# Four attention layers on one core: the max shifts of layers 0 and 2 are spread in another PSUM bank, kept twice, and the written-out order is renewed

## The chip, the cores and the metric

One core of a Trainium2 chip runs the whole program. The time is that of one execution on the device in microseconds; the result is the median of several. Beside it stands one profiled execution of the same kernel, whose trace gives every instruction's start and duration.

## The reference, cut to what matters

Thirty-two images of 128 channels by 1024 pixels pass through four layers, each of them attention over the pixels of one image:

```python
x = _L0_conv_ref(x, ...)   # group norm, one head of 128 channels, softmax over 1024 keys, residual
x = _L1_conv_ref(x, ...)   # group norm, eight heads of 16 channels, softmax, projection, residual
x = _L2_conv_ref(x, ...)   # instance norm, one head of 128 channels, softmax, residual
x = _L3_conv_ref(x, ...)   # linear attention, no softmax
```

Layers 0 and 2 ("full" layers, names with f) compute, for each image,

```python
attn = softmax(q k^T * C**-0.5)   # 1024 x 1024
out  = attn v
```

The softmax subtracts each query's largest score before the exponential. The change touches how that subtraction is done, not what it computes.

## The kernel before, in words

**Stages.** The work on one image is cut into 661 steps. Each step is a few instructions on one engine, and a step's name says its layer: g_ (norm of layer 0), f_ (layers 0 and 2, with the layer as last argument), p_ (norm and projections of layer 1), m_ (the maxima of layer 1), s_ (scores, exponential and values of layer 1), o_ (its division and projection), i_ (norm of layer 2), t_ (layer 3). TensorE, VectorE, ScalarE, GpSimd and the DMA queue of SyncE each play their own steps strictly in order.

**The order is written out by hand.** TIME has a number for every step, PERIOD (line 31) is the distance between two images, and a step of image i comes at i * PERIOD plus its number. STEPS_IN_ORDER sorts all of them once, and each engine takes its own steps out of that list (play). So in the steady state one period holds steps of four or five neighbouring images in a fixed interleaving, and the numbers act only through the order they give. What an engine really waits for is a semaphore in front of each step.

**The banks.** PSUM has eight banks, and each is given to one purpose: P_HEAD (two banks, a score tile of layer 1), P_MAX (two banks, the tiles whose maxima VectorE reduces, for layer 1 by m_max and m_max_read, for the full layers by f_max and f_max_read), P_ACC (values of layer 1), P_SC (score tiles of the full layers), P_FULL (values of the full layers) and P_CHAIN (everything short: projections, averages, spreads). Nothing is double-buffered: a tile can be written when the one before it has been read. P_CHAIN's readers are counted in the semaphore chain, by a table that is built from the order (CHAIN_READER, chain_free, chain_left).

**The full layers' shifts.** f_max computes a 128 x 1024 score tile for 128 queries, and f_max_read reduces it to one column of f0mx or f2mx. After four such columns f_shift (GpSimd, line 742) writes them on the diagonals of f_diag. f_base (TensorE) multiplies f_diag by a matrix of ones, which spreads the negated maxima of the 512 queries of one half over all partitions, into P_SC. f_based (VectorE, line 1087) copies that to f_shifts. Only then may f_scores write the first score tile of the half into the same bank. f_less (line 1107) adds f_shifts to a tile on its way to fp, f_exp (ScalarE, lines 892 and 894) takes the exponential twice, f_plo (GpSimd, line 760) makes the low part, f_add (lines 777 and 781) sums, and f_pv multiplies by the values. There are two halves (h = 0, 1) of eight tiles each (u = 0 to 15), for each of the two layers. The base of half 1 waits for the eighth f_less of half 0, since it overwrites both P_SC and the one f_shifts.

**The DMA queue** (SyncE) plays load, stack (six transfers that lay layer 1's q and k out by heads, one stack for each two pairs of heads), m_row, o_gather, o_move, o_return, f_gather, f_return and store, in order too; a transfer whose semaphore isn't reached holds up all behind it. f_out (GpSimd, line 787) writes x3 and waits for the store of the image before.

All matmuls of the program are recorded on line 1251, so the tiles tell them apart: p_sc<-f_diag,ones_r is f_base, p_sc<-f2q_hi,f2k_hi begins an f_scores of layer 2, p_chain<-zrow,ones_r is a spread of reciprocals, p_chain<-cw,t_dn is t_turn.

## Time and profile before

| | us |
|---|---|
| median of 3 runs | 6187.82 (6186.03 to 6192.17) |
| profiled execution, its time | 6179.77 |
| profiled execution, its span | 6178.0 |
| one period in the steady state (store to store, 27 of 31) | 182.3 to 183.2 |
| TensorE busy | 5741.7 (93%) |
| VectorE busy | 4620.2 (75%) |
| ScalarE busy | 4141.6 (67%) |
| GpSimd busy | 3426.0 (55%) |

TensorE's busy time is a union of modelled matmul durations: a matmul's record is longer than the distance to the next one, so waits shorter than that overlap are not visible as idle time. The distance from one record's start to the next is the better measure of what a step takes. The last periods are shorter (169, 147, 158 and 135 us), since fewer images are in flight.

### The profile page before, as it was taken

The page shows a single profiled execution, that of the slowest core. Times are in us where ns is not written, and L with a number is a line of the kernel's source. Part 1 is how long each engine was busy: PE and PEld are TensorE (multiplying, and loading weights), DVE is VectorE, ACT ScalarE, POOL GpSimd, SP SyncE. Part 2 cuts the span into 40 slices and gives each one's busy share as a digit, 9 for nine tenths or more (in the row PEclk, how much of TensorE's full clock was granted, in tenths as well). Part 3 has the DMA queues.
Part 4 walks back from the last instruction along what each step waited for, and adds up shares of the span by engine and source line. Part 5 has one row for each costly group of instructions (what it writes and reads, how often), then busy time and mean ns, then how long its engine had stood idle before and what let it go on. Part 6 is the DMA issues. An engine that isn't in the chain of part 4 may idle for free.

```text
span 6178.0 us, 82441 instructions
## 1 busy us (share of the span) xinstructions
PE 5741.7 (93%) x28818; PEld 2690.0 (44%) x28818; DVE 4620.2 (75%) x5748; ACT 4141.6 (67%) x5764; POOL 3426.0 (55%) x2739
## 2 busy tenths in 40 slices
PE   5789999999999999999999999999999999999885
PEld 2334444444444444444444444444444444444332
DVE  2677777777777777777777777777777777777752
ACT  2367777766777676777766767767677777677652
POOL 4336655556665555655555666555565555566433
PEclk7899999999999999999999999999999999999996
DMA  1011101011101101111101110110110110111000
GB/s 36 4 27 24 29 21 30 20 31 24 31 19 30 31 20 31 24 25 25 29 21 31 24 31 19 30 30 21 31 24 21 29 30 20 31 24 31 16 17 8
DMA packets 103485, 154.27 MB, mean 25 GB/s; under 512 B 63776, under 2 KB 66080, under 8 KB 102944
## 3 DMA queue, kind: packets, MB, share of 16 engines
q1 hardware_dynamic: 103072, 149.00, 11.1%
q8 instruction: 230, 3.77, 0.3%
q14 instruction: 183, 1.50, 0.1%
HBM read 18.13 MB, written 16.78 MB: 6 GB/s over the span
## 4 chain that ended last, share of the span: by engine, by line
PE 72%; DVE 16%; ACT 5%; issue 3%; POOL 3%; DMA 0%; SPq 0%; DVEq 0%; POOLq 0%; ACTq 0%
PE p_max L1251 16%; PE p_chain L1251 15%; PE p_sc L1251 12%; PE p_full L1251 11%; PE p_acc L1251 9%; PE p_head L1251 8%; DVE mx_half L1066 8%; ACT p L930 3%; DVE f2mx L1061 2%; DVE fp L1107 2%; POOL x L787 1%; POOL fsum L781 1%; POOL fp_lo L760 1%; DVE f_num L1125 1%; DVE t_dn L1198 1%
## 5 line engine op out<-in xcount | busy, mean ns | idle before, releaser
L1066 DVE TENSOR_REDUCE mx_half<-p_max 128x2 f32<-128x1024 f32 x2048 | 2506.8, 1224 | 891.1 <-PE p_max L1251 883.1
L930 ACT ACTIVATE p<-p_head 128x1024 f32<-128x1024 f32 x2048 | 2094.8, 1023 | 1103.0 <-PE p_head L1251 1047.8
L760 POOL TENSOR_TENSOR fp_lo<-fp,fp_hi 128x512 fp32r<-128x512 f32 x1024 | 1311.6, 1282 | 734.1 <-ACT fp L894 732.5
L781 POOL TENSOR_TENSOR fsum<-fsum,fp 128x512 f32<-128x512 f32 x768 | 987.9, 1286 | 282.3 <-ACT fp L894 282.1
L1251 PE MATMUL p_max<-ks,qs 63*128 63x512 f32 x4096 | 993.9, 481 | 102.0 <-DVE mx_half L1066 80.3
L1251 PE MATMUL p_acc<-p,v 128*17 128x512 f32 x8192 | 1080.9, 601 | 7.8 <-ACT p L930 7.6
L1251 PE MATMUL p_head<-qs,ks 64*128 64x512 f32 x4096 | 938.9, 454 | 43.6 <-ACT p L930 26.5
L892 ACT ACTIVATE fp_hi<-fp 128x512 fp32r<-128x512 f32 x1024 | 641.4, 626 | 367.3 <-DVE fp L1107 261.6
L1107 DVE TENSOR_TENSOR fp<-p_sc,f_shifts 128x512 f32<-128x512 f32 x1024 | 700.1, 684 | 147.5 <-PE p_sc L1251 60.3
L1251 PEld LDWEIGHTS p_max<-ks,qs 63*128 63x128 f32 x4096 | 385.8, 185 | 921.5 <-DVE mx_half L1066 736.3
L1251 PEld LDWEIGHTS p_head<-qs,ks 64*128 64x128 f32 x4096 | 385.7, 185 | 679.5 <-issue 385.8
L894 ACT ACTIVATE fp<-fp 128x512 f32<-128x512 f32 x1024 | 634.2, 619 | 0.0
L1061 DVE TENSOR_REDUCE f0mx<-p_max 128x1 f32<-128x1024 f32 x256 | 312.2, 1220 | 136.4 <-PE p_max L1251 136.2
L777 POOL TENSOR_TENSOR fsum<-fp 128x512 f32<-128x512 f32 x128 | 164.1, 1282 | 427.6 <-ACT fp L894 427.6
L1061 DVE TENSOR_REDUCE f2mx<-p_max 128x1 f32<-128x1024 f32 x256 | 312.5, 1221 | 104.2 <-PE p_max L1251 104.2
L1251 PEld LDWEIGHTS p_acc<-p,v 128*17 128x17 f32 x8192 | 144.6, 95 | 328.3 <-issue 282.2
L1251 PE MATMUL p_sc<-f2q_hi,f2k_hi 128*128 128x512 f32 x512 | 253.6, 495 | 35.0 <-DVE fp L1107 31.3
L1251 PE MATMUL p_sc<-f0q_hi,f0k_hi 128*128 128x512 f32 x512 | 251.0, 490 | 19.9 <-DVE fp L1107 17.9
L1251 PE MATMUL p_full<-fp_hi,f0v_hi 128*128 128x512 f32 x512 | 242.6, 474 | 2.7 <-POOL fp_lo L760 2.7
L1251 PE MATMUL p_full<-fp_hi,f2v_hi 128*128 128x512 f32 x512 | 228.7, 447 | 5.9 <-POOL fp_lo L760 5.9
L1251 PE MATMUL p_max<-f2k_hi,f2q_hi 128*128 128x512 f32 x512 | 187.7, 448 | 29.2 <-DVE f2mx L1061 17.4
L1251 PE MATMUL p_max<-f0k_hi,f0q_hi 128*128 128x512 f32 x512 | 185.2, 444 | 24.8 <-DVE f0mx L1061 17.2
(187 smaller groups left out, 7977.6 us busy)
## 6 DMA issues: line engine op xcount, KB each, us to landing
qs<-cq_hi SPq DMA_DIRECT2D x128, 256.0 KB, 4.8
ks<-ck_hi SPq DMA_DIRECT2D x128, 256.0 KB, 4.7
x_in<-x_dram SPq DMA_DIRECT2D x32, 512.0 KB, 4.4
qs<-cq_lo SPq DMA_DIRECT2D x64, 256.0 KB, 4.4
ks<-ck_lo SPq DMA_DIRECT2D x64, 256.0 KB, 5.1
out_dram<-x SPq DMA_DIRECT2D x32, 512.0 KB, 5.3
o<-o SPq DMA_DIRECT2D x256, 32.0 KB, 2.0
zrow<-rz SPq DMA_DIRECT2D x128, 16.0 KB
```

The lines of the kernel that those rows point to most:

```text
L760: pool.tensor_tensor(fp_lo[u % 2][:, :], fp[u % 2][:, :], f32(fp_hi[u % 2][:, :]), ALU.subtract).then_inc(f.plo, 1)
L777: pool.tensor_tensor(dst, fp[(u - 1) % 2][:, :], fp[u % 2][:, :], ALU.add)\
L781: pool.tensor_tensor(dst, dst, fp[u % 2][:, :], ALU.add).then_inc(f.sum, 1)
L787: pool.tensor_tensor(x3[:, :], f_num[:, :], x2[:, :], ALU.add)\
L892: act.activation(fp_hi[u % 2][:, :], fp[u % 2][:, :], ACT.Exp, scale=float(C) ** -0.5).then_inc(f.p, 1)
L894: act.activation(fp[u % 2][:, :], fp[u % 2][:, :], ACT.Exp, scale=float(C) ** -0.5).then_inc(f.pexact, 1)
L930: act.activation(p1[slot][:, 2 * pr:2 * pr + 2, :], P_HEAD[:, :].rearrange("p (e n) -> p e n", e=2), ACT.Exp, scale=float(DH) ** -0.5).the ...
L1061: dve.reduce_max(f_mx[layer][:, v:v + 1], P_MAX[:, :], AX.X).then_inc(sem.max_read, 1)
L1066: dve.reduce_max(mx_half[:, pr, :, t, kh], P_MAX[:, :].rearrange("p (e n) -> p e n", e=2), AX.X)\
L1107: dve.tensor_tensor(fp[u % 2][:, :], P_SC[:, :], f_shifts[:, :], ALU.add)\
L1125: dve.tensor_tensor(f_num[:, q], f_num[:, q], P_CHAIN[:, :], ALU.mult)\
L1251: return pe.matmul(dst, lhsT, rhs, start=start, stop=stop)
```

## The change

Five things are changed at once:

1. f_base writes P_CHAIN instead of P_SC, as one more user in that bank's turn, and f_based copies from there. The semaphore f_based is gone; chain takes its place.
2. f_shifts becomes two tiles, one for each half. The second lies on four weight matrices that are not read after the start (wp0, wp1, wp1a, wp1b; the list of matrices is reordered so that they are neighbours).
3. f_scores of a half's first tile no longer waits for the shifts. It waits, like the others, for the read of the tile before it. f_less of the first tile waits for the shifts.
4. f_base of half 1 no longer waits for the last f_less of half 0; f_based waits that its copy's readers in the layer before are done.
5. All numbers of TIME are new, and so is PERIOD; FIRST and FINAL become zero.

```diff
-PERIOD = 206.000
+PERIOD = 205.571
...
-    f_base=[-265.857, 261.032, -234.29, 310.141],
-    f_based=[-267.09, 255.678, -238.322, 303.472],
...
+    f_base=[189.564, 714.532, 231.86, 761.493],
+    f_based=[189.253, 709.867, 225.951, 758.072],
...
-                    f_spread="f_divide", o_spread="o_divide", o_project="o_residual",
+                    f_spread="f_divide", f_base="f_based", o_spread="o_divide", o_project="o_residual",
...
-FIRST = [-0.019, -0.019, -0.003]
-FINAL = [0.012, 0.017, 0.028]
+FIRST = [0.000, 0.000, 0.000]
+FINAL = [0.000, 0.000, 0.000]
...
-        f_shifts = sb("f_shifts", [C, HALF])
+        f_shifts = [sb("f_shifts", [C, HALF]), cw[:, COL["wp0"]:COL["wp0"] + HALF]]
...
             def f_based(b, h, layer):
                 f = full(layer)
                 dve.wait_ge(f.base, b.at(PER.f_base, h + 1))
-                dve.tensor_copy(f_shifts[:, :], P_SC[:, :]).then_inc(f.based, 1)
+                if layer == 0:
+
+                    after(dve, (sem.f2.less, b.shift(-3), PER.f_less, T * (h + 1)),
+                          (sem.f0.less, b.shift(-1), PER.f_less, T * (h + 1)))
+                else:
+                    after(dve, (sem.f0.less, b.shift(2), PER.f_less, T * (h + 1)),
+                          (sem.f2.less, b.shift(-1), PER.f_less, T * (h + 1)))
+                dve.tensor_copy(f_shifts[h][:, :], P_CHAIN[:, :]).then_inc(sem.chain, 1)
 
             def f_less(b, u, layer):
                 f = full(layer)
                 dve.wait_ge(f.sc, b.at(PER.f_sc, u + 1))
-                dve.wait_ge(f.based, b.at(PER.f_based, u // T + 1))
+                if u % T == 0:
+                    dve.wait_ge(sem.chain, chain_left("f_based", b, u // T, layer))
...
-                dve.tensor_tensor(fp[u % 2][:, :], P_SC[:, :], f_shifts[:, :], ALU.add)\
+                dve.tensor_tensor(fp[u % 2][:, :], P_SC[:, :], f_shifts[u // T][:, :], ALU.add)\
                    .then_inc(f.less, 1)
...
             def f_base(b, h, layer):
                 f = full(layer)
                 pe.wait_ge(f.shift, b.at(PER.f_shift, h + 1))
-                if h:
-                    pe.wait_ge(f.less, b.at(PER.f_less, T))
...
-                mm(P_SC[:, :], ones_r[:, :], f_diag[:, :, :].rearrange("p t c -> p (t c)"))\
-                    .then_inc(f.base, 1)
+                chain_free("f_based", b, h, layer)
+                mm(P_CHAIN[:, :], ones_r[:, :], f_diag[:, :, :].rearrange("p t c -> p (t c)"))\
+                    .then_inc(f.base, 1)
...
             def f_scores(b, u, layer):
...
-                if kt:
+                if u:
                     pe.wait_ge(f.less, b.at(PER.f_less, u))
-                else:
-                    pe.wait_ge(f.based, b.at(PER.f_based, h + 1))
```

The new numbers of TIME are the places 0 to 660 of an order, each used once in a period. What they move is seen in the order of the instructions, at three places that matter below. In all three, the first block is the kernel before and the second the changed one.

TensorE, where half 0 of layer 2 gets its shifts. From the second p_chain<-zrow,ones_r (the spread of reciprocals of layer 0) to the base:

```order
L1251 MATMUL p_chain<-zrow,ones_r 128x512
L1251 MATMUL p_max<-f2k_hi,f2q_hi 128x512 x2
L1251 MATMUL p_head<-qs,ks 128x512 x2
L1251 MATMUL p_acc<-p_0,v_1 17x512 x4
L1251 MATMUL p_head<-qs,ks 128x512 x2
L1251 MATMUL p_max<-f2k_hi,f2q_hi 128x512 x2
L1251 MATMUL p_sc<-f_diag,ones_r 128x512
```

```order
L1257 MATMUL p_chain<-zrow,ones_r 128x512
L1257 MATMUL p_head<-qs,ks 128x512 x2
L1257 MATMUL p_max<-f2k_hi,f2q_hi 128x512 x2
L1257 MATMUL p_sc<-f2q_hi,f2k_hi 128x512
L1257 MATMUL p_sc<-f2q_lo,f2k_hi 128x512
L1257 MATMUL p_sc<-f2q_hi,f2k_lo 128x512
L1257 MATMUL p_head<-qs,ks 128x512 x2
L1257 MATMUL p_acc<-p_0,v_1 17x512 x4
L1257 MATMUL p_max<-f2k_hi,f2q_hi 128x512 x2
L1257 MATMUL p_chain<-f_diag,ones_r 128x512
```

The first score tile of layer 2 (three matmuls), which came after the base with five other steps between, now lies ahead of it.

VectorE, where half 1 of layer 2 begins. The copy of its shifts (COPY f_shifts), the last maxima of layer 1 (mx_half, then mx), the first maxima of layer 0 of a later image (f0mx), the row of negated maxima for layer 1 (CAST neg), and the tiles 8 and 9 of layer 2 (fp):

```order
L1066 TENSOR_REDUCE mx_half<-p_max 128x2
L1087 COPY f_shifts<-p_sc 128x512
L1066 TENSOR_REDUCE mx_half<-p_max 128x2
L1075 TENSOR_TENSOR mx<-mx_half 128x2x2x8
L1061 TENSOR_REDUCE f0mx<-p_max 128x1 x2
L1107 TENSOR_TENSOR fp<-p_sc,f_shifts 128x512
L1061 TENSOR_REDUCE f0mx<-p_max 128x1
L1082 CAST neg<-p_chain 32x128
L1107 TENSOR_TENSOR fp<-p_sc,f_shifts 128x512
```

```order
L1064 TENSOR_REDUCE mx_half<-p_max 128x2
L1092 COPY cw<-p_chain 128x512
L1064 TENSOR_REDUCE mx_half<-p_max 128x2
L1113 TENSOR_TENSOR fp<-p_sc,cw 128x512
L1064 TENSOR_REDUCE mx_half<-p_max 128x2
L1059 TENSOR_REDUCE f0mx<-p_max 128x1
L1073 TENSOR_TENSOR mx<-mx_half 128x2x2x8
L1059 TENSOR_REDUCE f0mx<-p_max 128x1
L1113 TENSOR_TENSOR fp<-p_sc,cw 128x512
L1059 TENSOR_REDUCE f0mx<-p_max 128x1
L1080 CAST neg<-p_chain 32x128
```

The copy moved one reduction ahead, tile 8 moved ahead of the last reduction of layer 1, and tile 9 stands two instructions before CAST neg where it stood right behind it.

The DMA queue, from the load of an image to o_move (o_0<-o_1):

```order
L670 DMA zrow<-f0rz 1x128x8 x2
L614 DMA x_in<-x_dram 128x1024
L675 DMA out_dram<-x 128x1024
L634 DMA qs<-neg 2x16x128
```

```order
L659 DMA f2zt<-cw 128x1x8
L668 DMA zrow<-f2rz 1x128x8 x2
L673 DMA out_dram<-x 128x1024
L653 DMA zrow<-rz 4x32x32 x2
L644 DMA o_0<-o_1 16x512 x4
```

The store (out_dram<-x) stood behind the load and stands behind the return of layer 2's reciprocals (zrow<-f2rz). Everything else in the queue keeps its order.

Two more moves belong to layer 3. On TensorE five steps came between t_matrix (p_chain<-tm,ka) and t_ksum (p_chain<-cw,ma), and now two do. On VectorE tile 9 of layer 0 (fp) stood in front of t_scale (wb, t_dn, t_ds) and stands behind it and the reduction after it.

## Rows read from the trace of the kernel before

**Rows 1.** Page: busy time, share of the span, instructions of each engine

```profile
PE 5741.7 (93%) x28818; PEld 2690.0 (44%) x28818; DVE 4620.2 (75%) x5748; ACT 4141.6 (67%) x5764; POOL 3426.0 (55%) x2739
```

**Rows 2.** Busy time by stretch, one period: us, busy PE, PEld, DVE, ACT, POOL, PEclk, DMA

```profile
2992.40:3175.20 182.80, 176.01 (x903) 83.08 (x901) 144.35 (x181) 129.21 (x181) 106.78 (x86) 1.00 0.12 26
```

**Rows 3.** Who waited for whom: engine, line, releaser, us in total, times, longest

```profile
PEld p_max L1251 <- DVE mx_half L1066: 736.3, 1186, 1.8
...
PEld p_head L1251 <- ACT p L930: 284.1, 389, 1.7
```

**Rows 4.** Timeline of PE, layer 2's base of half 0 (start us, us, what [idle<-releaser])

```profile
3005.26 0.50 PE L1251 MATMUL p_chain<-zrow,ones_r 2*128 2x512 f32 x1
...
3008.52 0.73 PE L1251 MATMUL p_max<-f2k_hi,f2q_hi 128*128 128x512 f32 x2
...
3009.64 0.50 PE L1251 MATMUL p_sc<-f_diag,ones_r 128*128 128x512 f32 x1 [0.38 <-POOL f_diag L742]
...
3012.83 0.48 PE L1251 MATMUL p_sc<-f2q_hi,f2k_hi 128*128 128x512 f32 x1
...
3016.61 0.50 PE L1251 MATMUL p_sc<-f2q_hi,f2k_hi 128*128 128x512 f32 x1 [0.27 <-DVE fp L1107]
```

**Rows 5.** Timeline of DVE, the same stretch

```profile
3005.86 0.69 DVE L1125 TENSOR_TENSOR f_num<-f_num,p_chain 128x512 f32<-128x512 f32 x1 [0.21 <-PE p_chain L1251]
...
3012.26 1.22 DVE L1061 TENSOR_REDUCE f2mx<-p_max 128x1 f32<-128x1024 f32 x1 [0.37 <-PE p_max L1251]
...
3014.30 1.22 DVE L1061 TENSOR_REDUCE f2mx<-p_max 128x1 f32<-128x1024 f32 x1 [0.31 <-PE p_max L1251]
...
3015.86 0.69 DVE L1107 TENSOR_TENSOR fp<-p_sc,f_shifts 128x512 f32<-128x512 f32 x1
```

**Rows 6.** Busy time by stretch, the same stretch (columns as in Rows 2)

```profile
3004.43:3018.28 13.85, 13.02 (x67) 4.86 (x60) 12.74 (x21) 8.93 (x11) 2.85 (x3) 1.00 0.26 77
```

**Rows 7.** Timeline of PE, layer 2's tile 10

```profile
3064.27 0.50 PE L1251 MATMUL p_sc<-f2q_hi,f2k_hi 128*128 128x512 f32 x1 [0.53 <-DVE fp L1107]
```

**Rows 8.** Timeline of DVE, just before it

```profile
3060.95 1.23 DVE L1061 TENSOR_REDUCE f0mx<-p_max 128x1 f32<-128x1024 f32 x1 [0.22 <-PE p_max L1251]
3063.34 0.28 DVE L1082 CAST neg<-p_chain 32x128 fp32r<-32x128 f32 x1 [1.16 <-PE p_chain L1251]
3063.55 0.67 DVE L1107 TENSOR_TENSOR fp<-p_sc,f_shifts 128x512 f32<-128x512 f32 x1
```

**Rows 9.** Timeline of PE, layer 3

```profile
3126.08 1.83 PE L1251 MATMUL p_chain<-tm,ka 128*17 128x129 f32 x15
...
3131.06 0.39 PE L1251 MATMUL p_chain<-cw,ma 17*128 17x17 f32 x2
...
3134.21 1.05 PE L1251 MATMUL p_chain<-cw,t_dn 128*17 128x128 f32 x8 [0.68 <-DVE t_dn L1209]
```

**Rows 10.** Chain that ended last: one step of P_MAX's ring

```profile
3082.86 0.45 PE p_max L1251 x2
3083.33 1.24 DVE mx_half L1066
3084.61 0.51 PE p_max L1251 x2
```

**Rows 11.** Timeline of the DMA queue: return of layer 2, then a stack's last transfer

```profile
3096.74 1.17 SPq L670 DMA_DIRECT2D zrow<-f2rz  x2
...
3144.57 1.30 SPq L629 DMA_DIRECT2D ks<-ck_lo  x1
```

**Rows 12.** Timeline of POOL: f_out

```profile
3108.03 2.39 POOL L787 TENSOR_TENSOR x<-f_num,x 128x1024 f32<-128x1024 f32 x1 [0.34 <-DVE f_num L1125]
```

**Rows 13.** Page: a stack's transfers, KB each, us to landing

```profile
ks<-ck_lo SPq DMA_DIRECT2D x64, 256.0 KB, 5.1
```

**Rows 14.** Timeline of PE: the tile that waits for this stack

```profile
3151.05 0.50 PE L1251 MATMUL p_max<-ks,qs 63*128 63x512 f32 x2
```

**Rows 15.** One tile (x): transfers of 512 KB, issue to landing

```profile
DMA to landing us min/median/max: 2.6/5.3/5.7
```

More of the change, by code:

```diff
@@ L158 @@
-    o_return=[50.299, 119.226],
-    o_move=[88.54, 101.005],
-    o_spread=[215.825, 217.853],
-    o_divide=[215.329, 218.256],
-    o_project=[220.642, 226.102],
-    o_residual=[226.176, 228.408],
-    i_stat=[230.18],
-    i_apply=[235.791],
-    f_out=[374.775],
-    t_project=[371.091, 374.67, 375.592],
-    t_tokens=[372.077, 374.541, 377.951],
-    t_norms=[379.422],
-    t_keys=[380.954],
-    t_matrix=[390.878],
-    t_keep=[376.906],
-    t_ksum=[395.741],
-    t_scale=[390.327],
-    t_turn=[396.761, 400.053],
@@ new lines @@
+    p_lo=[309.61, 323.605, 323.916, 339.466],
+    p_value=[324.849, 328.581],
+    p_keep=[323.294, 325.16],
+    stack=[268.558, 339.155],
+    m_max=[378.652, 380.829, 383.006, 384.872, 386.738, 388.915, 391.092, 394.202, 396.69, 399.489,
[6 rows of a table added]
+    m_max_read=[374.92, 376.786, 377.097, 380.518, 381.451, 389.537, 390.47, 390.781, 396.068,
[6 rows of a table added]
+    m_both=[455.469, 555.611],
+    m_turn=[462.311, 572.716],
+    m_neg=[460.445, 561.831],
+    m_row=[362.791, 421.57],
+    s_scores=[465.11, 467.598, 470.086, 471.641, 473.818, 476.617, 478.794, 482.837, 485.014,
[6 rows of a table added]
@@ new lines @@
+    o_recip=[579.869, 666.327],
+    o_return=[499.631, 585.778],
+    o_move=[527.932, 568.051],
+    o_spread=[672.858, 674.102],
+    o_divide=[671.303, 676.59],
+    o_project=[676.901, 679.078],
+    o_residual=[683.121, 684.054],
+    i_stat=[684.987],
+    i_apply=[686.231],
+    f_out=[828.98],
+    t_project=[830.846, 833.645, 839.243],
+    t_tokens=[825.248, 832.09, 836.755],
+    t_norms=[841.109],
+    t_keys=[844.53],
+    t_matrix=[853.549],
+    t_keep=[846.085],
+    t_ksum=[856.97],
@@ L250 @@
     f_base = 2
-    f_based = 2
     f_less = 2 * T
@@ L325, in __init__ @@
         self.base = new(f"f{layer}_base")
-        self.based = new(f"f{layer}_based")
         self.less = new(f"f{layer}_less")
```

156 lines of the change are left out of this document (73 added, 83 removed), and 48 rows, old and new, of tables (m_max, m_max_read, s_exp, s_scores).

## The prediction

> **What bounds the kernel now.** I read the page first, for the shares [rows 1]: TensorE is busy 93% of the span, VectorE 75%, ScalarE 67%, GpSimd 55%. Then one steady period by itself [rows 2]: 182.8 us, TensorE busy 176.0, VectorE 144.4, ScalarE 129.2, GpSimd 106.8, at a granted clock of 1.00. TensorE's 176 is not all work, because a matmul's record runs on after the next has started: the scores of a full tile are three records of about 0.4 us that start 0.23 to 0.34 apart. So I looked at who waited for whom [rows 3]. The weight loads for p_max waited 736 us for VectorE's reductions and those for p_head 284 us for ScalarE's exponentials. The kernel is a fixed interleaving on TensorE with many small gaps (736 us in 1186 waits, 0.6 us each); a change in the order pays where it fills a gap, and costs where it opens one.
>
> No instruction goes and none comes: four bases, four copies and 32 score tiles for each image before and after. The copy reads 128x512 from one bank instead of another, and I take it at the same price. Everything is therefore waits. I went to the places where the old rule (the base sits in P_SC, the first tile waits for the copy) or the moved steps touch a visible gap.
>
> **Place one, the base of half 0 of layer 2.** The second spread starts at 3005.26 and the base at 3009.64 after an idle wait for GpSimd's f_diag; those 4.38 us are a chain through VectorE and GpSimd, not TensorE work [rows 4]. The first score tile starts at 3012.83, and the second only at 3016.61, after a wait for VectorE's fp. The changed order puts the first tile (three matmuls, 0.8 us from start to start) into the stretch before the base, where TensorE has time. That takes 0.8 us out of what follows. But VectorE is nearly full here: its gaps ahead of the first fp are 0.21, 0.37 and 0.31 us [rows 5], and over the 13.85 us around it VectorE is busy 12.74 [rows 6]. Only the last two gaps wait for tiles that TensorE now sends earlier, so at most 0.37 + 0.31 = 0.68 us can be had. I take **0.65 us**, the two idle waits of TensorE, 0.38 and 0.27 [rows 4]; from below 0.
>
> **Place two, tile 10 of layer 2.** It starts after an idle wait of 0.53 us for fp of tile 9 [rows 7]. VectorE stood idle 1.16 us in front of CAST neg, whose matmul was late, and fp was queued behind it [rows 8]. In the changed order fp comes two instructions ahead of the cast, and its score tile one value tile earlier, because the base of half 1 no longer has to wait for the bank and the single f_shifts. The wait goes: **0.53 us**; from below 0.
>
> **Place three, layer 3.** t_turn waits 0.68 us for t_dn [rows 9]. t_matrix starts at 3126.08 and t_ksum, which starts t_dn's chain, at 3131.06. With two steps between them instead of five, and with fp of tile 9 behind the chain instead of before it (0.68 us), t_dn is ready about 1 us sooner and the wait goes: **0.68 us**. The fp that was passed is needed by a tile some 10 us later, so the delay is covered; without that cover it would cost the chain's 2.7 us.
>
> **The other three bases** (both of layer 0, half 1 of layer 2) show no idle wait on TensorE, since many other steps lie between their maxima and their use; I count them at nothing. If a base now came before its f_diag, TensorE would wait as it does for half 0 of layer 2, 0.38 us each.
>
> **What the new order costs.** P_MAX is one tile deep. From one tile to the next is 0.47 + 1.28 = 1.75 us at best [rows 10], and TensorE needs that much other work in between. I added up, over the 80 pairs of neighbouring tiles of a period, how much work is missing by the steps' own start-to-start times. The sum is 5.8 us in the old order and 6.2 in the new one, 0.4 us more. The tiles of the full layers take 0.73 us instead of 0.50 [rows 4] and so ask for more; I take 0.7. The same count for p_head (1.55 us from tile to tile) gives 2.7 and 1.9, so 0.8 less. These are sums of separate shortfalls, most of which overlap with others. I let the P_MAX debit stand in full and take the p_head credit as nothing, because its exponentials are rarely what the next step in line waits for.
>
> **The sum.** 0.65 + 0.53 + 0.68 - 0.7 = 1.16 us an image; I take **1.0**, since a step that starts sooner meets the next fixed chain. Such chains are the stacks: the last transfer is issued at 3144.57 [rows 11] and lands 5.1 us later [rows 13], at 3149.7, and the tile that needs it starts at 3151.05 [rows 14], only 1.4 us of slack; the new order moves that tile one step forward. The places occur in all 32 images, but the first and the last are less crowded; I count 30: 30 us. On the profiled execution that is 6179.8 - 30 = 6150. The median of the runs stands 8 us above that execution, so against it I say 6187.8 - 30 = **6158 us**, 0.5% less. Bounds for this case: 0.4 us (12 us in all, 6176) if half of the gains meet other chains, and 1.9 (57 us, 6131) if the debit is nothing.
>
> **A rule beside the row.** The P_SC bank is held by base and copy for 0.50 + 0.68 us, four times an image, but it carries 32 tiles of about 1.7 us, some 60 us of 182.8 with the bases: it is idle two thirds of the time, so freeing it is worth no more than the waits above. The Trainium skill (PSUM — Partial Sum Buffer, "PSUM bank collisions raise a hardware error") says that two engines may not use one bank at once, in the same quadrant, and that software must keep them apart. By that rule alone all 4.7 us an image would be exclusion in TensorE's path and the change worth 140 us.
>
> **The rivals.**
> *Given back (0.22).* The waits move instead of going. Place one is limited by VectorE, place two's TensorE meets the f0mx tiles next, and m_max waits for a stack with little slack [rows 13, 14]. For it: VectorE's 12.74 of 13.85 us [rows 6]. Against: place three has nothing behind it. Net 0 to 0.3 us an image: 6180 to 6188.
> *P_MAX decides, slower (0.14).* In the new order a P_MAX tile follows another with only 0.9 us of work in between once (at layer 2's projections), and 1.0 once (f_max 5 to 6 of layer 2), where the least had been 1.1. The 736 us of waits for these reductions [rows 3] are 23 us an image, so this ring is the most waited for. If each shortfall counts and each pushes VectorE's later steps behind it once more, 2 x 0.7 = 1.4 us, and the three places give only 0.4: 1.0 us an image worse, 6218. It decides as soon as the added waits pass the 1.9 us of gains.
> *The store holds up f_out (0.03), slower.* The store now goes out after zrow<-f2rz, whose issue ends at 3097.9 [rows 11]; f_out waits for it and starts at 3108.03 [rows 12]. A 512 KB transfer lands after 5.3 us, at most 5.7 [rows 15]: 3103.6. There are 4.4 us to spare; each us beyond them would cost 30 us, since fp_lo stands behind f_out on GpSimd. A landing of 12 us would give 6158 + 2.3 x 30 = 6227.
> *Freed bank (0.03), much faster.* The exclusion of the rule above counts whole: 6050.
>
> The forecast has 0.58. A measurement of this kernel can tell about 0.2% (12 us) from no change. Faster by more than that is nearly all of the forecast and the freed bank, 0.59; within it 0.23; slower 0.18. The range takes in the forecast's bounds, all of "given back" with the runs' spread, and stops short of the P_MAX case: 6122 to 6203.
>
> **What would show it.** The base of half 0 of layer 2 as p_chain<-f_diag with the first score tile just before it, and the idle waits for f_diag and fp there gone or under 0.3 us. The 0.53 us wait ahead of tile 10 gone, and PE's 21 us of waits for t_dn near zero. A period of 181.5 to 182.2 us. Wrong would be: weight loads of p_max waiting over 750 us for mx_half (the P_MAX rival), f_out released by a DMA (the store), or the same gaps one step later (given back).

## The result and the profile after

| | us |
|---|---|
| median of 3 runs, before | 6187.82 |
| median of 3 runs, changed | 6114.58 (6112.51 to 6120.84) |
| ratio | 0.9883 [0.987, 0.9896], 73 us less |
| profiled execution, its time | 6120.84 (before 6179.77) |
| profiled execution, its span | 6119.0 |
| period in the middle of the run (first score tile of layer 1 to the next image's), median of 17 | 180.3 (before 182.8) |
| the same, mean | 180.58 (before 182.83) |

The forecast was 6158 with a range of 6122 to 6203. The direction was right and the size was not: 73 us came instead of 30, and the result lies 7 us outside the range.

The page of the changed kernel, busy time, against [rows 1]:

```profile
PE 5733.8 (94%) x28818; PEld 2703.8 (44%) x28818; DVE 4583.2 (75%) x5748; ACT 4154.7 (68%) x5764; POOL 3432.1 (56%) x2739
```

One period of it (columns as in [rows 2], TensorE first):

```profile
2939.78:3120.05 180.27, 175.23 (x901) 83.20 (x900) 142.79 (x180) 129.51 (x181) 106.92 (x86) 1.00 0.12 26
```

The same number of matmuls, at the same granted clock of 1.00, and nearly the same busy time: the 2.5 us are idle time that went. Who waited for whom (columns as in [rows 3]):

```profile
PEld p_max L1257 <- DVE mx_half L1064: 614.4, 1016, 1.8
PEld p_head L1257 <- ACT p L928: 331.9, 480, 2.1
...
PEld p_chain L1257 <- DMA zrow<-f2rz: 35.1, 31, 6.1
...
PE p_chain L1257 <- DVE t_dn L1215: 1.9, 1, 1.9
```

Weight loads for p_max waited 122 us less for VectorE than in [rows 3], those for p_head 48 us more for ScalarE, and a new wait for a DMA came, 35 us. TensorE's waits for t_dn are gone.

**Place one** (timeline of TensorE, columns as in [rows 4]). The first score tile now stands ahead of the base, and the base, in p_chain, starts without an idle wait. But a tile of P_MAX behind it now waits for VectorE, and the second score tile still waits for its fp:

```profile
2974.47 0.49 PE L1257 MATMUL p_chain<-zrow,ones_r 2*128 2x512 f32 x1
...
2975.89 0.40 PE L1257 MATMUL p_sc<-f2q_hi,f2k_hi 128*128 128x512 f32 x1
...
2978.86 0.50 PE L1257 MATMUL p_chain<-f_diag,ones_r 128*128 128x512 f32 x1
...
2982.76 0.73 PE L1257 MATMUL p_max<-f2k_hi,f2q_hi 128*128 128x512 f32 x2 [0.58 <-DVE f2mx L1059]
...
2985.83 0.50 PE L1257 MATMUL p_sc<-f2q_hi,f2k_hi 128*128 128x512 f32 x1 [0.26 <-DVE fp L1113]
```

From the second spread to the second score tile it is 11.36 us now and was 11.35 [rows 4]: place one gave nothing.

**Place two.** TensorE around half 1 of layer 2: the base, tile 8 right behind it, a projection of layer 0 (which writes p_chain too), tile 9 and tile 10:

```profile
3020.35 0.39 PE L1257 MATMUL p_chain<-f_diag,ones_r 128*128 128x512 f32 x1
...
3021.78 0.50 PE L1257 MATMUL p_sc<-f2q_hi,f2k_hi 128*128 128x512 f32 x1
...
3022.58 1.02 PE L1257 MATMUL p_chain<-x_in,cw 128*128 128x512 f32 x2
...
3028.04 0.39 PE L1257 MATMUL p_sc<-f2q_hi,f2k_hi 128*128 128x512 f32 x1
...
3032.36 0.40 PE L1257 MATMUL p_sc<-f2q_hi,f2k_hi 128*128 128x512 f32 x1
```

Tile 10 starts without the 0.53 us of [rows 7]. VectorE in the same stretch: the copy of the base, the subtraction of tile 8, that of tile 9, the cast neg, and the maximum behind it:

```profile
3021.17 0.68 DVE L1092 COPY cw<-p_chain 128x512 f32<-128x512 f32 x1
...
3023.09 0.69 DVE L1113 TENSOR_TENSOR fp<-p_sc,cw 128x512 f32<-128x512 f32 x1
...
3029.38 0.68 DVE L1113 TENSOR_TENSOR fp<-p_sc,cw 128x512 f32<-128x512 f32 x1
...
3031.47 0.28 DVE L1080 CAST neg<-p_chain 32x128 fp32r<-32x128 f32 x1
3032.56 1.23 DVE L1059 TENSOR_REDUCE f0mx<-p_max 128x1 f32<-128x1024 f32 x1 [0.81 <-PE p_max L1257]
```

In [rows 8] the cast came after an idle wait of 1.16 us and one subtraction stood between it and the next maximum. Now the cast has no wait before it.

**Place three.** t_matrix starts at 3094.56 and t_ksum at 3097.08, 2.5 us behind it instead of 5.0 [rows 9], and t_turn no longer waits.

```profile
3094.56 1.93 PE L1257 MATMUL p_chain<-tm,ka 128*17 128x129 f32 x16
...
3097.08 0.39 PE L1257 MATMUL p_chain<-cw,ma 17*128 17x17 f32 x2
```

**Where in the period the time went.** I followed TensorE's instructions through both traces by counting them in order, from the first score tile of layer 1 of an image. (s_scores(r, u) is score tile u, 0 to 15, of round r, 0 to 3; a round is four of the eight heads for one half of the queries.) Two orders can be compared only at points up to which both have issued the same instructions. Elsewhere a difference tells what moved and not what was gained: s_scores(1,14) is only 0.06 us earlier, because the changed kernel has the three matmuls of tile 8, 0.8 us, behind it by then and the kernel before has not. At points where the work done is the same (median of 17 images):

| up to | earlier by, us | of it since the row above |
|---|---|---|
| second spread, the start of place one | 0.27 | 0.27 |
| s_scores(1,2), behind place one | 0.27 | 0.00 |
| s_scores(1,12) | 0.73 | 0.46 |
| s_scores(2,0), behind place two | 1.32 | 0.59 |
| s_scores(3,2) | 1.31 | 0.0 |
| s_scores(3,7), ahead of the base of half 1 of layer 0 | 1.86 | 0.55 |
| s_scores(3,12), behind that base | 1.97 | 0.11 |
| s_scores(3,15), behind place three | 2.70 | 0.73 |

**The gains outside the three places.** The 0.46 and the 0.55 us come where TensorE stood idle before a tile of P_MAX until VectorE had reduced the one before it, and the new order sends another step first. Kernel before, then changed, for each of the two:

```profile
3035.72 0.50 PE L1251 MATMUL p_max<-ks,qs 63*128 63x512 f32 x2 [0.30 <-DVE mx_half L1066]
...
3114.98 0.50 PE L1251 MATMUL p_max<-ks,qs 63*128 63x512 f32 x2 [0.48 <-DVE mx_half L1066]
```

```profile
3004.57 1.05 PE L1257 MATMUL p_acc<-p,v 128*17 128x512 f32 x8
3005.56 0.50 PE L1257 MATMUL p_max<-ks,qs 63*128 63x512 f32 x2
...
3082.59 0.50 PE L1257 MATMUL p_head<-qs,ks 64*128 64x512 f32 x2
3082.93 0.41 PE L1257 MATMUL p_max<-ks,qs 63*128 63x512 f32 x2
```

A third wait of this kind, 0.33 us for f2mx, went from the stretch ahead of the second spread, where p_head now goes first. All three are there in each of the 17 images before, and in none after. The two gains are larger than the idle times shown by 0.1 to 0.2 us; that part is not traced. That the swaps make the gains is read from the traces; no run took one of them alone.

### The profile page after: what moved, and what is told of

The parts are those of the page before. It is cut to its first block, busy times and chain, and to the rows that moved or that the text cites. A ratio compares the mean times of both kernels' runs of the same rounds, so it can differ in the third digit from the quotient of the medians.

```text
span 6119.0 us, 81671 instructions
## 1 busy us (share of the span) xinstructions
PE 5733.8 (94%) x28818; PEld 2703.8 (44%) x28818; DVE 4583.2 (75%) x5748; ACT 4154.7 (68%) x5764; POOL 3432.1 (56%) x2739
## 4 chain that ended last, share of the span: by engine, by line
PE 76%; DVE 15%; ACT 3%; issue 2%; POOL 1%; DMA 1%; SPq 1%; POOLq 0%; DVEq 0%; ACTq 0%
PE p_chain L1257 17%; PE p_max L1257 16%; PE p_sc L1257 12%; PE p_full L1257 11%; PE p_acc L1257 11%; PE p_head L1257 9%; DVE mx_half L1064 8%; DVE f2mx L1059 3%; ACT p L928 2%; DVE fp L1113 1%; DVE f0mx L1059 1%; ACT exact L835 0%; DVE x L1163 0%; POOL fsum L779 0%; DVE f_num L1131 0%
## 5 line engine op out<-in xcount | busy, mean ns | idle before, releaser
L1257 PE MATMUL p_max<-ks,qs 63*128 63x512 f32 x4096 | 972.0, 471 | 79.5 <-DVE mx_half L1064 57.4
L1257 PE MATMUL p_head<-qs,ks 64*128 64x512 f32 x4096 | 966.0, 467 | 30.4 <-ACT p L928 17.9
L1113 DVE TENSOR_TENSOR fp<-p_sc,cw 128x512 f32<-128x512 f32 x512 | 349.2, 682 | 71.3 <-POOL fsum L779 30.3
L1113 DVE TENSOR_TENSOR fp<-p_sc,f_shifts 128x512 f32<-128x512 f32 x512 | 349.8, 683 | 53.4 <-PE p_sc L1257 29.3
```

The costliest lines, as they stand in the source:

```text
L1113: dve.tensor_tensor(fp[u % 2][:, :], P_SC[:, :], f_shifts[u // T][:, :], ALU.add)\
L1257: return pe.matmul(dst, lhsT, rhs, start=start, stop=stop)
```

## The experiments

All are the changed kernel or the one before with the edit shown; times are medians of 4 to 11 runs, ratios are to the kernel before on the same chip (6188 to 6192 us there). The f_ lists of TIME count layers fastest: index 2u is layer 0, 2u + 1 layer 2. A line TIME[...] = ... sets one step's number and so moves that step alone in the order.

### Rules and order apart

**new_rules_old_order**: the changed code with the old numbers. **old_rules_new_order**: the old code with the new numbers, and the first tile of half 0 of layer 2 behind its base again, which the old rule needs. **tile0_back**: the changed kernel with that same tile behind its base, so that it differs from old_rules_new_order in the rules alone.

```diff
+TIME["f_scores"][1] = TIME["p_average"][0] + 2 * PERIOD + 0.1
```

> The changed code with the old numbers (TIME, PERIOD, FIRST, FINAL). Theory A, that the gain of 73 us comes from where steps stand in the new order: the order is the old one, TensorE reaches the base and the first tiles at the old places, so the time stays within 10 us of before, 6178 to 6190. Rival B, that the freed bank and the second place for the shifts give the gain by themselves (waits that go whatever the order): 6130 or less. Between them, 6130 to 6178, both have a part.

> The old code (base in P_SC, one f_shifts, first tile waits for the copy) with the new numbers; only the first tile of layer 2 must stand behind the base again (after p_average), since the old rule cannot run otherwise. Theory A: the order keeps most of its gain without the new rules, at most 0.3 us an image lost for the first tile and 0.3 for half 1's base: 6125 to 6140. Rival B: without the rules the gain is gone, 6175 to 6190. A mixed answer would show a wait for the base or the copy that the old rule brings at half 1 of layer 2.

> The changed kernel with the first score tile of layer 2 back behind the base and p_average. My prediction gave this place 0.65 us an image, which would make it 6134. The changed trace shows only 0.3 us gained up to the end of this stretch, so theory A now says 8 us more, 6123. If VectorE really bounds the stretch, 6115 to 6118.

| | us | ratio |
|---|---|---|
| new rules, old order | 6228.27 | 1.0066 [1.0053, 1.0078] |
| old rules, new order | 6209.49 | 1.0033 [1.002, 1.0046] |
| tile0_back | 6118.77 | 0.9889 [0.9876, 0.9903] |

Neither theory had expected this: each half of the change alone is slower than the kernel before, by 39 and 20 us, and together they are 73 faster. tile0_back shows that place one's tile is worth nothing that can be told: 4 us between medians, on ranges that overlap (6115.54 to 6121.41, and 6112.51 to 6120.84), and its TensorE is at s_scores(1,2) as early as the changed kernel's. Between old_rules_new_order and tile0_back only the rules differ, by 91 us, and the starts differ in two places only: 1.16 us between s_scores(1,12) and (1,14), the base of half 1 of layer 2, and 1.35 us between (3,6) and (3,8), the base of half 1 of layer 0. These are two of the bases that I had counted at nothing. And at the points of equal work old_rules_new_order is as far ahead of the kernel before as the changed kernel is at s_scores(1,12), and it gains the same 0.55 us around (3,6): those gains come from the order alone.

### The second halves' waits

**half1_waits** puts the two waits of the old rule back into the changed kernel, for the second halves alone; bank and places stay.

```diff
                 chain_free("f_based", b, h, layer)
+                if h:
+                    pe.wait_ge(f.less, b.at(PER.f_less, T))
...
+                if u == T:
+                    pe.wait_ge(sem.chain, chain_left("f_based", b, 1, layer))
```

> The changed kernel with the old rule's two waits put back for the second halves alone: the base of half 1 waits for the subtraction of tile 7 of its layer, and the first score tile of half 1 waits for the copy of the base. Bank, two places for the shifts, order and first halves stay as changed. Theory A (the serial chain tile 7, base, copy, tile 8 is what the new rules remove, at the two second halves): 91 us over the changed kernel, 6200 to 6212, with the loss between score groups (1,12) and (1,14) (+1.2 us) and between (3,6) and (3,8) (+1.3 us). Theory B (it is the bank, or the copies' place): within 10 us of 6115.

6204.62 us, 1.0024 [1.0014, 1.0033]: 90 us over the changed kernel (87 by the ratios, which allow for the different chips), as theory A said, with +1.17 us up to (1,14) and +1.35 between (3,6) and (3,8). TensorE's timeline in it, base and tile 8, and VectorE's, the subtraction of tile 7 and the copy:

```profile
3062.62 0.47 PE L1257 MATMUL p_chain<-f_diag,ones_r 128*128 128x512 f32 x1 [0.88 <-DVE fp L1113]
...
3064.16 0.50 PE L1257 MATMUL p_sc<-f2q_hi,f2k_hi 128*128 128x512 f32 x1
```

```profile
3061.79 0.68 DVE L1113 TENSOR_TENSOR fp<-p_sc,f_shifts 128x512 f32<-128x512 f32 x1
3063.12 0.69 DVE L1092 COPY cw<-p_chain 128x512 f32<-128x512 f32 x1 [0.65 <-PE p_chain L1257]
```

Tile 7, its subtraction, base, copy, tile 8: in the new order these stand close together, and under the old rule each waits for the one before. So the two waits alone cost some 90 us in the new order; what the bank as such is worth there is too little to tell (this run and old_rules_new_order are 5 us apart).

### Why the new rules lose in the old order

new_rules_old_order falls behind by 1.54 us in one place, between s_scores(1,12) and (1,14):

```profile
3073.99 0.50 PE L1257 MATMUL p_chain<-f_diag,ones_r 128*128 128x512 f32 x1
3075.74 1.13 PE L1257 MATMUL p_chain<-x_in,cw 128*128 128x512 f32 x2 [1.25 <-DVE cw L1092]
```

The base is now one more user of P_CHAIN, and the old order has f_qk(3) of layer 0 right behind it, which writes the same bank and has to wait for the copy. Two repairs were tried. **base_behind_qk** swaps the two; **base_early** puts the base behind tile 7 and the copy behind its subtraction.

```diff
+TIME["f_base"][3] = TIME["f_qk"][6] + 3 * PERIOD + 0.01
```

```diff
+TIME["f_base"][3] = TIME["f_scores"][15] + 0.01
+TIME["f_based"][3] = TIME["f_less"][15] + 0.01
```

> The changed code in the old order (6228.3) with one step swapped: the base of half 1 of layer 2 behind the layer-0 step f_qk(3) that stood right behind it on TensorE. Theory A (the old order with the new rules is slow because f_qk(3), which writes the chains' bank too, now waits for VectorE's copy of the base, 1.5 us an image): 6184 to 6190. Theory B (the loss is in the turns of the chains' bank elsewhere, or in the extra waits of the copy): 6215 to 6230.

> The changed code in the old order (6228) with the base of half 1 of layer 2 and its copy moved forward: base right behind tile 7 on TensorE, copy right behind the subtraction of tile 7 on VectorE, so that the copy is done before f_qk(3) needs the chains' bank. Theory A (the 1.55 us an image that the new rules lose in the old order is the turn of that bank, which the swap with f_qk(3) only handed on, from a wait for the copy to a wait for f_hi(3)): 6183 to 6192. Theory B (another cost of the rules in this order): 6215 to 6230.

base_behind_qk: 6224.81 us, 1.0058 [1.0046, 1.0071]; theory A's number failed. The swap only hands the wait on, since the base now waits for ScalarE's read of f_qk(3):

```profile
3076.27 0.47 PE L1257 MATMUL p_chain<-f_diag,ones_r 128*128 128x512 f32 x1 [1.45 <-ACT exact L835]
```

base_early: 6185.64 us, 0.9994 [0.9985, 1.0003], no different from the kernel before. So the bank's turn was the whole loss, and the new rules in the old order are worth nothing in themselves.

### Place three

**layer3_back**: t_ksum behind five steps again, and the subtraction of tile 9 of layer 0 ahead of layer 3's chain.

```diff
+TIME["t_ksum"][0] = TIME["f_pv"][14] + 3 * PERIOD + 0.1
+TIME["f_less"][18] = TIME["m_max_read"][24] - PERIOD + 0.1
```

> The changed kernel with t_ksum behind the score tile and value tile that it had been moved ahead of, and tile 9 of layer 0 ahead of t_scale again on VectorE. In the changed trace layer 3's stretch of the period is about 1.1 us shorter than before. Theory A: the wait for t_dn comes back (0.5 to 0.7 us idle on TensorE, 15 to 25 us in all in the trace), and the time rises by 1.1 x 30 = 33 us, to 6148. Rival (the shortening has other causes): under 10 us more, 6115 to 6125.

6149.91 us, 0.9942 [0.9928, 0.9955]: 35 us over the changed kernel, 1.2 us an image by my 30 images. The wait for t_dn is back:

```profile
PE p_chain L1257 <- DVE t_dn L1215: 28.9, 30, 1.9
```

### Place two, from the new order

**tile9_back** undoes one step on VectorE, the subtraction of tile 9 ahead of the cast. **second_half_back** puts tiles 8 and 9 and their subtractions back. **turn_back** moves only m_turn(1), the matmul that the cast reads, behind f_max(3).

```diff
+TIME["f_less"][19] = TIME["m_neg"][1] + PERIOD + 0.1
```

```diff
+TIME["f_scores"][17] = TIME["f_value"][0] + 3 * PERIOD + 0.1
+TIME["f_less"][17] = TIME["f_max_read"][2] + 3 * PERIOD + 0.1
+TIME["f_scores"][19] = TIME["f_pv"][15] + 0.1
+TIME["f_less"][19] = TIME["m_neg"][1] + PERIOD + 0.1
```

```diff
+TIME["m_turn"][1] = TIME["f_max"][6] + 2 * PERIOD + 0.1
```

> The changed kernel with the subtraction of tile 9 of layer 2 put back behind m_neg on VectorE; nothing else moves. Theory A (my term for place two, 0.53 us an image, stands or falls with this step, but in the new order tile 9 is issued 2.8 us earlier and can wait): 6115 to 6132. Theory B (this step is the whole gain of 1.25 us at place two): 6145 to 6155.

> The changed kernel with tiles 8 and 9 of layer 2 put back where the order before had them: tile 8 behind f_value(0) of layer 0, tile 9 behind the sum of tile 7, and their subtractions behind f_max_read(1) and m_neg. Theory A (my term: 0.53 us an image): 6128 to 6134. Theory B (the whole of place two hangs on these tiles being early, 1.25 us an image): 6148 to 6156. If neither, up to 6125, the gain lies with the other steps moved there.

> The changed kernel with one step moved: m_turn(1) behind f_max(3) on TensorE, as before the change. Theory A (m_neg then runs later and holds f_max_read(3) behind it on VectorE): f_max_read(3) 0.6 to 1.0 us later, 6132 to 6145. Theory B (only the subtraction of tile 9 behind m_neg costs, as in tile9_back): 6110 to 6122.

| | us | ratio | loss against the changed kernel |
|---|---|---|---|
| tile9_back | 6140.71 | 0.9924 [0.9911, 0.9936] | 26 |
| second_half_back | 6192.46 | 1.0004 [0.9995, 1.0013] | 78 |
| turn_back | 6181.26 | 0.9986 [0.9977, 0.9995] | 67 |

By the ratios the losses are 25, 75 and 64 us. tile9_back fell between the theories and the other two lost more than either allowed. The losses do not add up: moving two tiles back gives back all that the whole change gained. turn_back shows why one step weighs so much. Of its 2.3 us an image only 0.56 come where m_turn stands; 1.7 come some 11 us later, at o_recip(0). Its timeline of the DMA queue, then of VectorE:

```profile
3063.98 0.61 SPq L632 DMA_DIRECT2D qs<-neg  x1
...
3070.68 1.21 SPq L637 DMA_DIRECT2D zt<-o  x1
```

```profile
3063.67 0.28 DVE L1080 CAST neg<-p_chain 32x128 fp32r<-32x128 f32 x1 [1.15 <-PE p_chain L1257]
...
3074.62 0.35 DVE L1144 RECIPROCAL rz<-zt 128x32 f32<-128x32 f32 x1 [0.61 <-DMA zt<-o]
3075.01 1.15 DVE L1147 CAST rz<-rz 128x32 fp32r<-128x32 f32 x1
3076.19 1.21 DVE L1149 TENSOR_TENSOR rz<-rz 128x32 fp32r<-128x32 f32 x1
3077.33 1.21 DVE L1064 TENSOR_REDUCE mx_half<-p_max 128x2 f32<-128x1024 f32 x1
```

The cast is followed on the DMA queue by the row (qs<-neg), the six transfers of a stack and the gather (zt<-o), issued 6.7 us behind the row; the reciprocal starts 4.0 us after the gather's issue. The chain takes 11.0 us in all three kernels: as medians the cast stands at 93.02, 91.65 and 92.87 us of the period before, after and in turn_back, and the reciprocal at 104.06, 102.64 and 103.85. VectorE plays in order, so m_max_read(0) of the next image waits behind it: 105.54, 103.78 and 106.50. So the wait at the cast is also the start of a chain over SyncE's queue that ends in VectorE. In turn_back the reciprocal is 1.2 us later than in the changed kernel; the other 1.5 us up to m_max_read(0) are the two instructions behind it, 1.15 and 1.21 us long here and 0.2 in most images of the changed kernel (see the last section).

This prices the step in the new order. It is no gain on top against the kernel before: the changed kernel is 1.32 us ahead at s_scores(2,0), before the reciprocal, and 1.32 us ahead at (2,8), behind it. The cast had to come forward with the rest, or the gain would have been lost there.

### Is the long copy on the path?

The copy in the middle of o_recip(0) took 0.93 us on the mean in the kernel before (0.38 to 1.06) and 0.18 in the changed kernel, apart from 2 of 21 images with 1.17 and 1.31. **recip_behind_before** moves o_recip(0) of the old kernel one step later, behind m_max_read(0), clear of GpSimd in most images; **recip_behind_after** moves that of the changed kernel behind m_max_read(1).

```diff
+TIME["o_recip"][0] = TIME["m_max_read"][0] + PERIOD + 0.01
```

```diff
+TIME["o_recip"][0] = TIME["m_max_read"][1] + PERIOD + 0.01
```

> The kernel before with o_recip(0) one step later on VectorE, behind m_max_read(0). In the kernel before, the 128x32 copy in o_recip(0) takes 0.93 us on the mean while GpSimd is at a 128x512 sum, against 0.18 us in the changed kernel where GpSimd idles; behind m_max_read(0) it falls into a hole of VectorE (0.6 us) and mostly clear of GpSimd. Theory A (that lengthened copy is part of what the change took off the path at the end of place two): m_max_read(0) starts 0.4 to 0.7 us earlier, 6165 to 6182. Theory B (the copy's length is not on the path): 6186 to 6196.

> The changed kernel with o_recip(0) two steps later on VectorE, behind m_max_read(1), where GpSimd idles in most periods. In the changed kernel o_recip(0)'s copy takes 0.18 us in most periods and 1.2 to 1.3 in those in which GpSimd starts early; those periods are the ones of 181 to 182 us among the 180.2. Theory A: those long periods go, 6104 to 6112. Theory B (the hole behind m_max_read(1) is too short for the three steps, and they push the maxima that follow): 6114 to 6125.

```profile
3077.02 0.34 DVE L1138 RECIPROCAL rz<-zt 128x32 f32<-128x32 f32 x1
3077.40 0.18 DVE L1141 CAST rz<-rz 128x32 fp32r<-128x32 f32 x1
```

These two rows are VectorE's timeline in recip_behind_before: the copy took 0.18 us in each of the same 21 images, but the time was 6188.90, 1.0002 [0.9993, 1.0011]. The 0.75 us were not on the path there; theory A fell. recip_behind_after took 6114.16 us, 0.9882 [0.9868, 0.9895], as the changed kernel. Its mean period fell from 180.58 to 180.33 us, too little for the runs to tell.

### Place two, from the old order

If the place's own steps make the gain, putting them alone into the old order (new rules, base_early) must give it. Each kernel adds to the one before it:

- **tile8_early**: tile 8 ahead of f_qk(3), its subtraction ahead of m_max_read(63).
- **second_half_early**: tile 9's subtraction behind the first maxima, m_turn(1) and s_scores(1,15) ahead of f_max(3), two exponentials earlier.
- **second_half_whole**: what that left out on TensorE, VectorE and ScalarE.
- **second_half_four**: GpSimd's steps there as well, and s_scores(1,13) ahead of tile 7.

The first block is tile8_early's addition, the second some of what the other three add:

```diff
+TIME["f_scores"][17] = TIME["s_scores"][29] + PERIOD + 0.01
+TIME["f_less"][17] = TIME["m_max_read"][62] + PERIOD + 0.01
```

```diff
+TIME["m_turn"][1] = TIME["f_pv"][15] - PERIOD + 0.01
+TIME["f_less"][19] = TIME["f_max_read"][2] + 3 * PERIOD + 0.01
...
+TIME["f_exp"][15] = TIME["f_hi"][6] + 3 * PERIOD - 0.01
...
+TIME["f_add"][15] = TIME["f_vlo"][0] + 3 * PERIOD - 0.01
```

> As base_early, and tile 8 of layer 2 goes ahead of f_qk(3) on TensorE and its subtraction ahead of m_max_read(63) on VectorE, some 5 us earlier; everything else in the old order. Theory A (what the change gains at the second half of layer 2 is that one subtraction leaves VectorE's dense run of maxima, which sets the pace there): 0.6 to 1.4 us an image under base_early, 6145 to 6170. Theory B (the gain needs the whole new order): within 10 us of base_early.

> The changed code in the old order, with all that the new order does at the second half of layer 2 and nothing else of it: base and copy early as in base_early, tile 8 early as in tile8_early, tile 9 and its subtraction behind the first f_max steps instead of in front of m_neg, m_turn(1) and s_scores(1,15) ahead of f_max(3), and ScalarE's exponentials of tiles 8 and 9 each one step earlier. Theory A (place two's gain is that f_max_read(3) is no longer queued behind m_neg and a subtraction, 0.9 to 1.3 us an image, and tile 8 early only makes room for that): 6145 to 6160, against 6185.6 of base_early and 6204.2 of tile8_early. Theory B (it needs the rest of the new order too): over 6175.

> second_half_early with the steps that it left out: the sum of tile 6 ahead of f_max(1), m_both(1) behind f_max_read(0), the subtraction of tile 10 ahead of f_max_read(4), the exponential of tile 7 ahead of f_hi(3) and that of tile 10 ahead of s_out(1) on ScalarE; so TensorE, VectorE and ScalarE do the second half of layer 2 in the new order, and the rest in the old. Theory A (place two's gain needs its own steps on three engines and nothing else): 6145 to 6160, and m_neg some 1.3 us earlier than in base_early. Theory B (it needs what comes before it in the new order as well): over 6175.

> second_half_whole with GpSimd's part as well: the low half of p and the sum of tiles 6 and 7 of layer 2 ahead of the low halves of layer 0's projections and values, as in the new order, and on TensorE s_scores(1,13) ahead of tile 7. On all four engines the steps around the second half of layer 2 then stand as in the changed kernel, everything else as before. In second_half_whole the subtraction of tile 9 waited until 91.88 us of the period (89.60 in the changed kernel) for GpSimd's sum of tile 7, which stood behind f_vlo(0). Theory A (the gain at place two needs its steps on all four engines, and nothing elsewhere): s_scores(2,0) 1.0 to 1.4 us earlier than before, 6145 to 6160. Theory B (it also needs the earlier part of the period): over 6175.

| | us | ratio |
|---|---|---|
| base_early | 6185.64 | 0.9994 [0.9985, 1.0003] |
| tile8_early | 6204.19 | 1.0026 [1.0016, 1.0037] |
| second_half_early | 6211.95 | 1.0037 [1.0023, 1.0051] |
| second_half_whole | 6215.23 | 1.0043 [1.003, 1.0056] |
| second_half_four | 6162.56 | 0.9961 [0.9948, 0.9975] |

The first step made it 19 us slower, the next two did not help (8 and 3 us more, little over the spread), and the last gave 53 us at once. In second_half_whole the subtraction of tile 9 stands where the new order has it, but GpSimd's sum of tile 7, whose buffer it needs, still stands behind a low part of layer 0's values. VectorE's timeline, then GpSimd's:

```profile
3072.06 0.69 DVE L1113 TENSOR_TENSOR fp<-p_sc,cw 128x512 f32<-128x512 f32 x1 [1.48 <-POOL fsum L779]
```

```profile
3069.42 1.30 POOL L750 TENSOR_TENSOR f0v_lo<-exact,f0v_hi 128x512 fp32r<-128x512 f32 x1 [0.52 <-ACT exact L867]
3070.66 1.30 POOL L779 TENSOR_TENSOR fsum<-fsum,fp 128x512 f32<-128x512 f32 x1
```

In second_half_four the sum comes first, and the subtraction has no wait before it. VectorE's timeline again, then GpSimd's:

```profile
3048.24 0.68 DVE L1113 TENSOR_TENSOR fp<-p_sc,cw 128x512 f32<-128x512 f32 x1
```

```profile
3045.41 1.30 POOL L779 TENSOR_TENSOR fsum<-fsum,fp 128x512 f32<-128x512 f32 x1
3047.16 1.29 POOL L750 TENSOR_TENSOR f0v_lo<-exact,f0v_hi 128x512 fp32r<-128x512 f32 x1 [0.44 <-ACT exact L867]
```

Against the kernel before, at the points of equal work, second_half_four is 0.02 us ahead at s_scores(1,12) and 0.61 at (2,0): 0.59 us gained in between, as much as the changed kernel gains there. So the place's steps on four engines do make that gain, with nothing of the rest of the new order. Theory A had expected more, 1.0 to 1.4 us at (2,0) and 28 to 43 us in the time; it was 0.6 and 25. The last step moved GpSimd's steps and one of TensorE's together; that GpSimd's sum is what counts is read from the wait of 1.48 us that went.

### The new wait for a DMA

The return of layer 2's reciprocals is issued later in the new order, and the spread waits for it, 35 us in all. **row_early** moves the row and the reciprocal forward, **spread_later** moves the spread and its division back.

```diff
+TIME["f_row"][1] = TIME["f_exp"][0] + 3 * PERIOD - 0.05
+TIME["f_recip"][1] = TIME["m_max_read"][10] + 2 * PERIOD + 0.1
```

```diff
+TIME["f_spread"][1] += 0.7
+TIME["f_divide"][1] += 0.35
```

> The changed kernel with f_row(2) ahead of the exponential of tile 0 of layer 0 on ScalarE, and f_recip(2) ahead of the subtraction of tile 1 on VectorE, so that the row is returned some 1.6 us earlier. Theory A (the wait for the returned row, 1.0 us an image, is on the path): 6085 to 6100. Theory B (the next wait takes its place): 6110 to 6120.

> The changed kernel with f_spread(0) of layer 2 two steps later on TensorE (behind s_scores(3,1) and m_max(14)) and its division behind m_max_read(14). Theory A (the new wait for the returned row, 1.0 us an image, is on the path): 6085 to 6100. Theory B (the wait is cover for one that comes next, the P_MAX ring): 6110 to 6120.

row_early: 6115.77 us, 0.9883 [0.9869, 0.9896]; spread_later: 6122.65, 0.9894 [0.9881, 0.9908]. In row_early the wait is gone but for the last image:

```profile
PEld p_max L1257 <- DVE mx_half L1064: 618.4, 1030, 1.8
...
PEld p_chain L1257 <- DMA zrow<-f2rz: 6.1, 1, 6.1
```

The time stayed. The weight loads for p_max waited 4 us longer, in 14 more waits; which wait took the other 25 us I did not find. No kernel of the study is faster than the changed one by more than the runs can tell.

## Why the prediction was wrong

**"I let the P_MAX debit stand in full" is the step that failed: the sum took 0.7 us off, and these waits gave time back.** The weight loads for p_max waited 614 us for mx_half instead of 736, and TensorE's idle waits ahead of three tiles of P_MAX (0.33, 0.31 and 0.48 us an image) went. The stretches around them gave 0.27, 0.46 and 0.55 us, 1.3 us an image, none of it in a place of the sum. Adding up how much work is missing between neighbouring tiles came out 0.4 us worse for the new order, against what happened. It counts the work that stands between two tiles, and says nothing of work that is itself waiting, nor of which shortfall TensorE really stands idle for. That the swaps of neighbours make these gains is read from the traces, and old_rules_new_order has them too; which swap gives how much was not tried. I looked for gains only where the old rule or the listed moves touch a wait, and the new order had closed gaps elsewhere. The count for p_head pointed the wrong way too: it promised 0.8 us less, and its waits rose by 48 us.

**Place one, 0.65: nothing.** Between the second spread and the second tile the time is 11.36 us for 11.35. The wait for f_diag went and a wait of 0.58 us for f2mx came. I had named the reason, VectorE's 12.74 of 13.85 us [rows 6], and taken the upper end all the same.

**Place two, 0.53: 0.59 us, right in place and size.** The wait ahead of tile 10 went, and second_half_four makes the same 0.59 us from this place's steps alone. What the term did not have is how many steps on four engines must stand right for it, and that the late cast also starts the chain to the reciprocal: in the new order one of these steps back costs 26 or 67 us. The reason given, that the base of half 1 no longer has to wait, holds: half1_waits loses 1.17 us here.

**Place three, 0.68: 0.73 us in the trace, 1.2 by layer3_back.** The wait for t_dn went. Why putting it back costs more than it gave stays open; how much each of its two steps does was not tried.

**"The other three bases ... I count them at nothing".** Against the kernel before this is right, and for the reason given: base_early shows that the new rules, placed well in the old order, are worth nothing. But it looked at the old order only. In the new one tile 7, base, copy and tile 8 stand close together, and under the old rule they would be a chain that costs 1.2 and 1.35 us an image, some 90 us in all (half1_waits). The new rules do not add to the sum; without them all that the order gives is lost.

**The sum.** As forecast 0.65 + 0.53 + 0.68 - 0.7 = 1.16, taken as 1.0. As measured 0 + 0.59 + 0.73 at the three places, 1.28 at the gaps of P_MAX and 0.1 elsewhere: 2.7 us by the last score tile. The median period is 2.5 us shorter and the mean 2.26, since some periods of the changed kernel are longer than 180.3 (see the last section). The three places together gave 1.3 us where I had 1.9; that this is not far from my 1.0 is luck, since the debit between the two did not exist. Taking 30 images was near enough (73 / 2.26 = 32; the two profiled executions, one below its median and one above, are 59 us apart).

**The rivals.** P_MAX decides: fell with its waits. The store: fell; GpSimd's f_out waited for VectorE's f_num in all 32 images, never for a DMA. (Its price had a slip: a landing of 12 us is 1.9 us beyond what there was to spare, not 2.3, which makes 6215.) Given back: true of place one and of the new wait for the row, wrong as a whole. The freed bank at 6050: half1_waits keeps base and copy out of P_SC and still takes 6205 us, so that what counts is the waits and where they stand; no run shows a price for the exclusion as such.

## What to carry to other kernels

When a change relaxes a rule and renews the order, look through the whole new order for waits that it fills, not only where the rule bites: nearly half of the gain came from swaps of neighbours that have nothing to do with the rule. And look in the new order for the places that the old rule would have tied; each half by itself tells nothing, and here each was slower. Compare two orders only at points where the engine has done the same work. Where engines play fixed orders, a place is one step on every engine that touches its buffers: with three engines' steps moved the kernel was 26 us slower than before, with the fourth's (and one more of TensorE's) 25 us faster. And follow a late instruction to all that it releases, DMA queues too, before moving it.

## What the runs showed of the hardware

**A small VectorE copy can last until GpSimd's instruction ends.** The copy in the middle of o_recip(0), 128x32 from and to SBUF, takes 0.18 us beside an idle GpSimd. In the kernel before it started at 3074.70 and took 1.00, to 3075.70, and GpSimd's sum ran to 3075.65. VectorE's timeline, then GpSimd's:

```profile
3074.70 1.00 DVE L1141 CAST rz<-rz 128x32 fp32r<-128x32 f32 x1
3075.73 0.19 DVE L1143 TENSOR_TENSOR rz<-rz 128x32 fp32r<-128x32 f32 x1
```

```profile
3074.38 1.27 POOL L781 TENSOR_TENSOR fsum<-fsum,fp 128x512 f32<-128x512 f32 x1
```

The Trainium skill (SBUF — State Buffer, "SBUF: two separate sides") says that VectorE and GpSimd share one pair of ports as an exclusive lock, held for the whole instruction, for VectorE instructions in a two-port mode, or with two SBUF inputs against a GpSimd instruction that reads SBUF. The trace agrees: the copy was long in all 21 images looked at of the kernel before, where a GpSimd instruction ran at its start each time, and in the changed kernel it was long in the 2 of 21 where one did and short in the 19 where none did. Two of the three periods of 182 us among the 17 fall on the images in which the copy was long (1.31 and 1.17 us). Whether such a copy costs anything depends on the order: nothing in recip_behind_before, while in turn_back two long ones (1.15 and 1.21) and a cast 1.2 us later together cost 1.7 us an image at that point.

**Two large transfers back to back.** The 512 KB store landed 2.9 us after its issue at the median, where it had been 5.3 before [rows 15]; in the old order its issue stood behind that of a load, also of 512 KB. Whether that is the reason was not tried.

```profile
DMA to landing us min/median/max: 2.6/2.9/5.1
```
